# A four-layer transformer kernel: its eight stand-alone norm phases rewritten for tiles of 512 tokens

## The reference

```python
def _layernorm(x, axis=-1, eps=1e-05):
    m = jnp.mean(x, axis=axis, keepdims=True)
    v = jnp.var(x, axis=axis, keepdims=True)
    return (x - m) / jnp.sqrt(v + eps)

mod = (_silu(c) @ wmod).reshape(c.shape[0], 6, 1, -1)
sa, ca, ga, sb, cb, gb = (mod[:, k] for k in range(6))
h = _layernorm(x, axis=-1) * (1 + ca) + sa
x = x + ga * attn(h)
h = _layernorm(x, axis=-1) * (1 + cb) + sb
x = x + gb * ffn(h)
```

## Time and profile before

| | us |
|---|---|
| times of three runs | 3821.44, 3792.84, 3825.76 |
| median | 3821.44 |
| span of the profiled execution, first to last instruction | 3792.6 |
| TensorE busy | 2747.7 |
| VectorE busy | 2269.6 |
| ScalarE busy | 1329.9 |
| GpSimd busy | 1103.8 |

### The profile page before, as it was taken

The page is one execution under the profiler, slowest core; times in us unless marked ns, Lnnn a source line. Parts: engine busy times, 40 slices in busy tenths (PEclk is TensorE's granted clock), DMA queues, the critical chain, the costliest instruction groups (busy, mean ns, idle before and its releaser), DMA issues. The chain is left out here.

```text
span 3792.6 us, 71700 instructions
## 1 busy us (share of the span) xinstructions
PE 2747.7 (72%) x20731; PEld 1822.0 (48%) x20756; DVE 2269.6 (60%) x5526; ACT 1329.9 (35%) x3004; POOL 1103.8 (29%) x1121
## 2 busy tenths in 40 slices
PE   4778624228788887878499966777799964568899
PEld 3555523216566666367255554555544631145344
DVE  4666672148788875322477755555555689965555
ACT  1555201005555553333166623444322221123321
POOL 2222107743333332646322222222100144421000
PEclk6999856558999998889599977888899965579899
DMA  3332302334334321355211102222000000000000
GB/s 70 42 43 35 120 34 56 45 75 60 50 42 53 42 33 50 122 120 101 65 25 24 20 14 36 35 35 27 27 1 0 1 3 0 0 6 23 4 0 22
DMA packets 154624, 148.12 MB, mean 39 GB/s; under 512 B 29433, under 2 KB 135554, under 8 KB 149378
## 3 DMA queue, kind: packets, MB, share of 16 engines
q1 hardware_dynamic: 118882, 121.52, 16.7%
q0 software_dynamic: 34336, 21.83, 4.0%
q10 hardware_dynamic: 1152, 1.61, 0.1%
HBM read 52.70 MB, written 33.01 MB: 23 GB/s over the span
## 5 line engine op out<-in xcount | busy, mean ns | idle before, releaser
L549 ACT ACTIVATE a1PR<-bank 128x384 f32<-128x384 f32 x512 | 242.9, 493 | 152.8 <-PE bank L607 149.3
L784 DVE TENSOR_REDUCE a1NM<-bank 128x3 f32<-128x384 f32 x512 | 263.1, 549 | 30.9 <-PE bank L589 27.9
L784 DVE TENSOR_REDUCE a4NM<-bank 128x3 f32<-128x384 f32 x256 | 132.8, 550 | 140.8 <-PE bank L589 139.0
L787 DVE TENSOR_REDUCE a2NMQ<-bank 128x2 f32<-128x512 f32 x256 | 168.1, 685 | 64.7 <-PE bank L593 64.4
L784 DVE TENSOR_REDUCE a0NM<-bank 128x3 f32<-128x384 f32 x256 | 134.1, 551 | 96.9 <-PE bank L589 95.6
L549 ACT ACTIVATE a4PR<-bank 128x384 f32<-128x384 f32 x256 | 122.2, 490 | 190.5 <-PE bank L607 190.1
L953 PE MATMUL bank<-ONES 128*128 128x256 bf16 x960 | 170.0, 284 | 23.5 <-DMA f3nWR<-in_wr 4.0
L549 ACT ACTIVATE a2PR<-bank 128x512 f32<-128x512 f32 x256 | 149.6, 596 | 99.3 <-PE bank L611 97.2
L1509 POOL TENSOR_TENSOR lM<-lF,lV 128x1024 f32<-128x1024 f32 x32 | 122.2, 3818 | 168.3 <-DVE lF L1522 167.8
L549 ACT ACTIVATE a0PR<-bank 128x384 f32<-128x384 f32 x256 | 121.9, 490 | 136.1 <-PE bank L607 135.6
L605 PE MATMUL bank<-a1QH,a1KH 128*128 128x128 bf16 x512 | 117.2, 230 | 56.1 <-ACT a1PR L549 42.1
(11 more groups left out here) (676 smaller groups left out, 8668.5 us busy)
## 6 DMA issues: line engine op xcount, KB each, us to landing
yWT<-in_w SPq DMA_DIRECT2D x40, 256.0 KB, 3.2
a1QH<-a1SPL SPq DMA_DIRECT2D x96, 64.0 KB
a1KH<-a1SPL SPq DMA_DIRECT2D x96, 64.0 KB
a1QH<-a1QH SPq DMA_DIRECT2D x96, 64.0 KB
a1KH<-a1KH SPq DMA_DIRECT2D x96, 64.0 KB
rows_by_slot<-gZB SPq DMA_DIRECT2D x5, 1040.0 KB
yXG<-rows_by_slot SPq DMA_DIRECT2D x40, 130.0 KB, 3.2
sums<-rZT SPq DMA_DIRECT2D x2, 2112.0 KB
```

What stands on the lines that cost most here:

```text
L549: nc.scalar.activation(PR[:, h % 8, :], bank[2 + h % 2][:, 0:NC], ACT.Exp, scale=SCALE)\
L784: v.tensor_reduce(NM3[:, h, :], S_BANK[h % 3][:, 0:NC].rearrange("p (n k) -> p n k", n=3), AX, ALU.max, negate=True).then_inc(s_used.sem, 1)
L787: v.tensor_reduce(NMQ[:, :, h], S_BANK[h % 3][:, 0:NC].rearrange("p (n k) -> p n k", n=2), AX, ALU.max, negate=True).then_inc(s_used.sem, 1)
```

## The change

`norm_phase` is written anew; its callers stay. A tile is now F = 512 tokens (two batches), so NG = 8 tiles. Centring is one product with identity minus 1/128 (`c.CEN`), whose result stays in PSUM (three banks in turn). ScalarE squares from there, one product with the full `c.MEAN` gives the variance of every token on all 128 partitions at once, ScalarE takes Sqrt of it with eps as its bias (`SD`), and VectorE takes the reciprocal of all 128x512 values (`RS`) and multiplies (`XN`). Gain and shift of the first batch are done by ScalarE (`h0`), of the second by VectorE (`h1`), both straight into the target. Logits for four groups of 128 tokens follow. The powers on GpSimd, the diagonals, the filler products and the loop are gone, and the small loads are awaited where they are first used. The attention phases keep their norms.

The diff, cut; what it removes from `norm_phase` is in the code above:

```diff
@@ -29,7 +29,8 @@
 
 
 C_ID, C_MEAN, C_TRI, C_COS, C_SIN = 0, 128, 256, 384, 640
-C_END = C_SIN + T
+C_CEN = C_SIN + T
+C_END = C_CEN + P
...
+    c[:, C_CEN:C_CEN + P] = np.eye(P) - 1.0 / D
...
+        self.EPS = self.sb("EPS", [P, 2])
...
+            nc.gpsimd.memset(c.EPS[:, 0:1], 1e-5).then_inc(const_ready, 1)
+            nc.gpsimd.memset(c.EPS[:, 1:2], 1.1920928955078125e-07).then_inc(const_ready, 1)
...
+    F, NG = 2 * T, NB // 2
+    CEN_BANK, VAR_BANK, LG_BANK = bank[0:3], bank[3:5], bank[5:7]
+    EPS = c.EPS[:, 0:1] if cfg["neps"] == 1e-5 else c.EPS[:, 1:2]
...
-        XC, SQ, XN = sb("XC", [P, 4, T]), sb("SQ", [P, 2, T]), sb("XN", [P, T])
-        H = sb("H", [P, 4, T])
-        VE, RS, DG = sb("VE", [P, 2, 2]), sb("RS", [P, 2, 2]), sb("DG", [P, 2, 2, P])
+        SQ, SD, RS, XN = sb("SQ", [P, 2, F]), sb("SD", [P, 2, F]), sb("RS", [P, F]), sb("XN", [P, 2, F])
         COL, WR = sb("COL", [P, 2]), sb("WR", [P, max(E, 1)])
-        S = signals(c, n_mean=int(centered), n_xc=int(centered), n_sq=1, n_var=1, n_ve=1, n_rs=1, n_dg=1, n_bc=1, n_xn=1,
-                    n_h=1, n_copied=1, n_logits=int(E > 0), n_lg=int(E > 0))
-        mean, xc, sq, var, ve, rs, dg, bc, xn, hr, copied, logits, lg = S
+        S = signals(c, n_cen=int(centered), n_sq=1, n_var=1, n_sd=1, n_rs=1, n_xn=1, n_h0=1, n_h1=1, n_logits=int(E > 0), n_lg=int(E > 0))
+        cen, sq, var, sd, rs, xn, h0, h1, logits, lg = S
...
-                step(t, t % 4)
+
+        def gains(b):
+            if cfg.get("ngain"):
+                return COL[:, 0:1], (COL[:, 1:2] if cfg.get("nshift") else 0.0)
+            l, k = cfg["layer"], cfg["nmod"]
+            return c.MOD[:, l, k + 1, one(b)], c.MOD[:, l, k, one(b)]
...
         @block.tensor
         def _(pe):
...
+            for t in range(NG + 3):
+                g = t
+                if centered and g < NG:
+                    after(pe, xn, g - 3)
+                    pe.matmul(CEN_BANK[g % 3][:, :], c.CEN, SRC[:, tok(g, F)], start=True, stop=True).then_inc(cen.sem, 1)
+                g = t - 1
+                if 0 <= g < NG:
+                    after(pe, sq, g)
+                    after(pe, sd, g - 2)
+                    pe.matmul(VAR_BANK[g % 2][:, :], c.MEAN, SQ[:, g % 2, :], start=True, stop=True).then_inc(var.sem, 1)
+                g = t - 3
+                if E and 0 <= g:
+                    if g == 0:
+                        pe.wait_ge(w_in, 16 * len(loads))
+                    after(pe, h0, g)
+                    after(pe, h1, g)
+                    after(pe, lg, g - 2)
+                    for n in range(4):
+                        mm = pe.matmul(LG_BANK[g % 2][:, n * E:(n + 1) * E], NT[:, g * F + n * P:g * F + (n + 1) * P], WR[:, :],
                                        start=True, stop=True)
                     mm.then_inc(logits.sem, 1)
...
-            steps(pe, step)
-
-        @block.gpsimd
-        def _(pool):
...
         @block.scalar
         def _(act):
-            def step(t, m):
...
+            for t in range(NG + 2):
+                g = t
+                if g < NG:
                     if centered:
-                        after(act, xc, t)
-                    after(act, var, t - 2)
-                    nc.scalar.activation(SQ[:, m % 2, :], XC[:, m, :] if centered else SRC[:, tok(t)], ACT.Square).then_inc(sq.sem, 1)
-                if has(-4, t):
-                    after(act, hr, t - 4)
-                    nc.scalar.copy(NT[:, tok(t - 4)], H[:, m % 4, :]).then_inc(copied.sem, 1)
-            steps(act, step)
+                        after(act, cen, g)
+                    after(act, var, g - 2)
+                    nc.scalar.activation(SQ[:, g % 2, :], CEN_BANK[g % 3][:, :] if centered else SRC[:, tok(g, F)], ACT.Square)\
+                        .then_inc(sq.sem, 1)
+                g = t - 1
+                if 0 <= g < NG:
+                    after(act, var, g)
+                    after(act, rs, g - 2)
+                    nc.scalar.activation(SD[:, g % 2, :], VAR_BANK[g % 2][:, :], ACT.Sqrt, bias=EPS).then_inc(sd.sem, 1)
+                g = t - 2
+                if 0 <= g:
+                    if g == 0 and loads:
+                        act.wait_ge(w_in, 16 * len(loads))
+                    after(act, xn, g)
+                    scale, shift = gains(2 * g)
+                    nc.scalar.activation(NT[:, tok(2 * g)], XN[:, g % 2, 0:T], ACT.Identity, bias=shift, scale=scale).then_inc(h0.sem, 1)
 
...
         @block.vector
         def _(v):
...
+            for t in range(NG + 2):
+                g = t
+                if g < NG:
+                    after(v, sd, g)
+                    after(v, xn, g - 1)
+                    v.reciprocal(RS[:, :], SD[:, g % 2, :]).then_inc(rs.sem, 1)
+                    after(v, rs, g)
+                    after(v, h0, g - 2)
+                    after(v, h1, g - 2)
+                    v.tensor_tensor(XN[:, g % 2, :], CEN_BANK[g % 3][:, :] if centered else SRC[:, tok(g, F)], RS[:, :], ALU.mult)\
+                        .then_inc(xn.sem, 1)
+                    if g == 0 and loads:
+                        v.wait_ge(w_in, 16 * len(loads))
+                    after(v, xn, g)
+                    scale, shift = gains(2 * g + 1)
+                    v.tensor_scalar(NT[:, tok(2 * g + 1)], XN[:, g % 2, T:F], scale, shift, ALU.mult, ALU.add).then_inc(h1.sem, 1)
+                g = t - 2
+                if E and 0 <= g:
+                    after(v, logits, g)
+                    v.tensor_copy(LG[:, 4 * g:4 * g + 4, 0:E], LG_BANK[g % 2][:, 0:4 * E].rearrange("p (n e) -> p n e", n=4)).then_inc(lg.sem, 1)
+    close(c, S, NG)
```

More of the change, by code:

```diff
@@ L102, in __init__ @@
         self.MEAN = self.CST[:, C_MEAN:C_MEAN + P]
+        self.CEN = self.CST[:, C_CEN:C_CEN + P]
     def sb(self, name, shape, dt=F32, ctx=None):
@@ L922, in norm_phase @@
             + ([(COL[:, 1:2], cfg["nshift"])] if cfg.get("nshift") else []) + ([(WR[:, :], cfg["wr"])] if E else [])
-        has = lambda stage, t: not isinstance(t, int) or 0 <= t + stage < NB
-        def steps(eng, step):
-            for t in range(8):
-                step(t, t % 4)
-            with eng.Fori(0, 2) as i:
-                for k in range(8, 12):
-                    step(i * 4 + k, k % 4)
-            for t in range(16, NB + 4):
-                step(t, t % 4)
+        def gains(b):
[3 more added lines that the diff above has]
+            return c.MOD[:, l, k + 1, one(b)], c.MOD[:, l, k, one(b)]
         block = ctx.enter_context(nc.Block())
@@ L944, in _ @@
         def _(pe):
-            if loads:
-                pe.wait_ge(w_in, 16 * len(loads))
-            spare = c.ONES[:, :].bitcast(BF16)
-            def busy(n):
-                for _ in range(n):
-                    pe.matmul(bank[7][:, 0:2 * P], spare[:, 0:P], spare[:, :], start=True, stop=True)
-            def step(t, m):
-                busy(2)
-                if has(0, t) and centered:
-                    after(pe, xc, t - 2)
-                    pe.matmul(bank[m % 2][:, 0:T], c.MEAN, SRC[:, tok(t)], start=True, stop=True).then_inc(mean.sem, 1)
-                if has(-3, t):
-                    b, d = t - 3, (m - 3) % 2
-                    after(pe, dg, b)
-                    after(pe, xn, b - 2)
-                    for n in range(2):
-                        mm = pe.matmul(bank[4 + d][:, n * P:(n + 1) * P], c.ONES[:, :], DG[:, d, n, :], start=True, stop=True)
-                    mm.then_inc(bc.sem, 1)
-                busy(2)
-                if has(-1, t):
-                    d = (m - 1) % 2
-                    after(pe, sq, t - 1)
-                    after(pe, ve, t - 3)
-                    for n in range(2):
-                        mm = pe.matmul(bank[2 + d][:, n:n + 1], SQ[:, d, n * P:(n + 1) * P], c.MEAN[:, 0:1], start=True, stop=True)
-                    mm.then_inc(var.sem, 1)
-                busy(2)
-                if E and has(-4, t):
-                    b = t - 4
-                    after(pe, hr, b)
-                    after(pe, lg, b - 1)
-                    for n in range(2):
-                        mm = pe.matmul(bank[6][:, n * E:(n + 1) * E], H[:, m % 4, n * P:(n + 1) * P], WR[:, :],
@@ L982, in step @@
                                        start=True, stop=True)
                     mm.then_inc(logits.sem, 1)
-            steps(pe, step)
-        @block.gpsimd
-        def _(pool):
-            def step(t, m):
-                if has(-1, t):
-                    d = (m - 1) % 2
-                    after(pool, ve, t - 1)
-                    after(pool, dg, t - 3)
-                    nc.gpsimd.tensor_tensor(RS[:, d, :], VE[:, d, :], c.HALF[:, 0:2], ALU.pow).then_inc(rs.sem, 1)
-            steps(pool, step)
@@ L996, in _ @@
         @block.scalar
         def _(act):
-            def step(t, m):
-                if has(0, t):
+            for t in range(NG + 2):
+                g = t
+                if g < NG:
                     if centered:
```

(10 more changed lines are left out.)

41 lines of the change are left out of this document (removed).

## The result

| | us | runs |
|---|---|---|
| kernel before, median | 3795.68 (3773.66 to 3825.76) | 20 |
| changed kernel, median | 3819.43 (3810.86 to 3832.45) | 20 |
| ratio | 1.0061, 95% interval 1.0042 to 1.0081 | |
| span of the profiled execution, before and after | 3792.6 and 3812.5 | |

What follows compares the result with a forecast made beforehand. VectorE, mainly its 512-column reciprocal, was taken to bound the new norm phases. Phases +37 us, table loads +1, experts of `f4` +2 and router phases +3 made +43 on 3821: 3864 us, range 3824 to 3905.

Steps and rivals of the forecast that it cites:

- the copies of the logits: Router phases: VectorE copies logits ahead of the next reciprocal, adding 1.4 us a phase, 2.7 in `f0n`.
- the starts: Phase start to first reciprocal: 7.2 us in most phases, 5.1 in `h3n`, 6.9 in `i3n`, 3.8 in `f2n`.
- The level: Base time that the shift was added to: 3821 us, the median of three runs, with 3792.8 the lowest.
- What bounds a tile: Norm phases: VectorE is the bound, with reciprocal 3.35 us, `XN` 0.69 and `h1` 0.41, over TensorE's 2.0 to 4.2.
- The beat: VectorE's time for a tile of 512 tokens in the norm phases: 4.57 us, 4.5 in `f2n`.
- The ends: Phase end: 0.15 us of ScalarE's half plus 0.27 to the next phase; routers add about 1.3, `f0n` 1.5.
- Behind the phases: After the norm phases: table loads +1 us, and the experts of `f4` without warm filler ahead +2.
- 3 us in all: Router phases: allowance for TensorE at the low clock, about 6.2 us a tile over VectorE's 4.8.
- TensorE as the bound: Rival: without filler the low clock returns, costing 34 us in `f0n`, `f1n`, `f3n`, less 3 counted: 3895 us; chance 10%.
- A short reciprocal: Rival: VectorE does a long row like a product, 0.69 us, so a phase takes 24 us: 3704 us; chance 5%.
- a dearer one: Rival: a reciprocal column takes eight passes of 1.04 ns, 4.4 us each, 67 us more: 3931 us; chance 8%.
- Cheaper starts: Rival: clock up early and smaller gaps save up to 2 us a phase: +20 to +37, 3841 to 3858 us; chance 17%.

Runs made afterwards that it cites:

- the version with columns: Changed kernel with the variance as one column per 128 tokens, Sqrt and reciprocal on 128x4, spread by TensorE products: 3744.34 us, 0.9867 of the kernel before.

## Why the prediction missed

Direction and mechanism held; the shift was too large by 19 us (43 for 24), and the level by 25. Both together put the forecast 45 us too high, but the range was missed by the shift alone: its low end, 3824, was +31 on the lowest run of three, and the shift came out as +24. The steps of the sum that failed are the gap counted between independent operations of VectorE with the copies of the logits counted in full, the starts, and what was put behind the phases. Point by point:

**The level (failed, -25 us).** The step "I put the shift on the median: 3821" took the median of three runs for the kernel's. Twenty runs have 3796; 3793 was the typical one of the three, and 3821 and 3826 were the slowest two of the twenty. On 3796 the same sum gives 3839. (In the executions of the kernel before whose time and span are both known, the time is 1.9 to 2.5 us above the span, so the profiled execution, with a span of 3792.6, took some 3795 us and is probably none of the three; the sum moves by 2 us with it.) Where the spread comes from is partly seen: over the executions profiled here the time outside the eight norms lies between 3464 and 3483 us, mostly in the stretch from `f1n` to `h2n` (the experts of layer 1 and the attention of layer 2: 680 to 697 us), which no kernel here changes. One thing goes with the kernel's own spread: of 41 executions of the kernel before, measured beside the experiments, the ten above 3810 us have a mean granted clock of 0.825 to 0.831, the 26 up to 3794 us one of 0.830 to 0.841. What makes the clock differ is open.

**What bounds a tile (held).** VectorE sets the beat in all eight phases; its reciprocal was forecast at 3.35 us and measured at 3.34, the product at 0.69, `h1` at 0.41.

**The beat (mis-sized, 4.57 for 4.44).** "Between dependent operations the timeline shows 0.04 us, three times 0.12" gave a gap to the step from `h1` to the next reciprocal too. Those two do not depend on each other, and the second starts 0.09 us before the first ends. That is 0.13 x 56 = 7 us over the seven intervals of each of the eight phases. The copies of the logits are of the same kind: in `f1n` the beat is (1505.30 - 1473.68) / 7 = 4.52, only 0.08 above that of a plain norm where 0.23 x 6/7 = 0.20 were counted; with `f0n` (0.25 for 0.39) and `f2n`, 4 us. Together the middle of the phases is 11.2 us short of the sum.

**The starts (mis-sized, -3.8 us).** 7.2 was forecast where 6.7 to 6.8 came in `f0n`, `f1n`, `h2n` and `f4n`: "centring of tiles 0 and 1 at 2.1 each" rounded up what the earlier trace rows had as 3.75 for two. `i3n` and `f3n` started in 5.4 and 5.7, as part of their first products ran at the high clock (the first four records in 3.46 and 2.68 us, the next in 1.02 and 1.91), `h3n` in 6.2 instead of 5.1, as part of its own did not (3.19 us, in spite of the busy experts ahead). `f2n` was right at 3.8.

**The ends (mis-sized, +3.9 us).** Plain norms end as forecast (4.96 us from the last reciprocal, 4.98 forecast). The router phases take 0.8 to 1.2 us more: the last logits run at the low clock, 1.87 us for the eight records that were put at 1.0.

These three make -11.1 us: 348.3 measured against 359.4 forecast for the phases, so +26 instead of +37.

**Behind the phases (+6 forecast, about +2 seen).** The table loads stick out by 0.34 us ahead of `uPB` and 0.6 ahead of `f2cPB`, as forecast; that of `a4` ends at 2287.8, 5 us before its Exp (2292.86), and costs nothing. The experts of `f4` begin with

```profile
3417.28 3.50 PE L1281 MATMUL bank<-f4NT,f4W 128*128 128x512 f32 x4 [13.55 <-DMA f4eFB<-in_hb]
```

where before it was

```profile
3398.40 1.96 PE L1321 MATMUL bank<-f4NT,f4W 128*128 128x512 f32 x4 [2.77 <-DMA f4eFB<-in_hb]
```

and the stretch to `f3n` grows by 1.1 us, half of the 2 forecast. The prediction's "being full all the time it should not stay there" is not what the runs show: in the old form without filler `f1n` and `f3n`, 95% busy, stayed at the low clock to the end. In the changed kernel it did not matter. The "3 us in all" for TensorE as the bound of a router phase did not come: VectorE never waits between tiles.

Together 26 + 2 = 28 us at the places that the change touches, against a difference of medians of 24 (interval 16 to 31). The two profiled spans differ by 19.9 us only: outside the norm phases the changed kernel's execution is 6 us shorter (3464.5 against 3470.5), so 8 us shorter where nothing was changed, 3 of them from `f1n` to `h2n` alone. That is luck of these two executions.

**The rivals.** A short reciprocal and a dearer one are ruled out by the line through six lengths up to 512 columns, 6.25 ns a column, six times the copy's slope of 1.04. The Trainium skill's repeat count of 8 (VectorE: DVE Perf Modes, "First, the fixed hardware budget"), taken as the price of a column, is what the dearer one stood for; the trace agrees with six. TensorE as the bound did not happen; in the old form without filler and in the version with columns it did, in the phases named above. Cheaper starts came true for 4 us. The measured shift lies in that rival's band (+20 to +37), but only in part for its reason: the overlap on VectorE, worth more, is a source that no rival named. Taking away the table switches gives 4 us; a load begins 0.01 us after the Square ahead of it ends (2196.73 + 0.60, 2197.34), and the Exps start 0.01 us behind their loads: 1.28 us with no drain stands. The Trainium skill (ScalarE: Activation LUTs, "What ACT_TABLE_LOAD costs") has 1.38 us of drain for each; no run here shows it.

## What to carry to other kernels

Before an operation is moved to an engine, count its columns and its price for one: powers of 128x2 values for each 256 tokens became a reciprocal of 128x512 for 512, and its 3.3 us outweighed every instruction, wait and hop that the new form saved. Where a value is the same over a dimension, do the dear function on the small shape and let TensorE spread the result: here that turned 0.6% slower into 1.3 to 1.8% faster than the kernel before. And do not take the middle one of three runs that lie 1% apart for the level: that the profiled execution lay near the median of twenty was luck too.

## What the runs showed of the hardware

Independent operations on VectorE overlap in the timeline: the reciprocal starts 0.09 us before the recorded end of `h1` ahead of it (2203.48 + 0.41, then 2203.80), while dependent ones stand 0.03 to 0.04 us apart (2202.75 + 0.69, then 2203.48). A small copy of 0.18 us between them lengthens the beat by 0.08. A float32 reciprocal on 128 partitions takes 153 ns and 6.25 ns a column, from 8 to 512 columns (198, 253, 353, 553, 1744, 3344 ns).

A busy TensorE does not by itself get the high clock. It was busy 91 to 98% of a phase and stayed at 0.50, 1.2 of 2.4 GHz, to the end (`f1n` and `f3n` of the old form without filler, `f2n` of the version with columns, with and without one filler at a place), while three fillers at each place brought 0.95 in the last of these. The old `h3n` without filler, busy 85%, had 0.84, and the old `f0n`, busy 88%, had 0.78. The rows don't say why; filler has to be tried in more than one amount and judged by the granted clock of the stretch.
